# Decoder layer in fp32 on one core: both attentions and the first experts issued in an order written call by call, with the last softmax weighting on POOL

## The reference

```python
x = x + attn(layernorm(x))          # 16 heads of 8, groups of 32 tokens, causal, q and k with rms norm
x = x + xattn(layernorm(x), ctx)    # own layer norm, 16 heads of 64, 64 context rows per batch, w_out, tanh(gate)
x = x + moe(layernorm(x))           # 16 experts of width 128, top 4 of the best 2 of 4 groups, 2 shared experts
# moe: y_e = (silu(x @ gate_e) * (x @ up_e)) @ down_e, weighted by the routing and summed over e
```

## Time and profile before

| | us |
|---|---|
| median of 3 runs | 193.97 (193.88 to 194.04) |
| the profiled execution | 193.8 |
| its span | 192.1 |
| PE busy | 176.5 (92%) |
| DVE busy | 141.4 (74%) |
| POOL busy | 120.1 (63%) |
| ACT busy | 107.6 (56%) |

### The profile page before, as it was taken

How to read it: one execution, slowest core, us unless ns; L and a number is a source line. 1 busy time by engine, 2 the same in 40 slices (tenths; PEclk the granted TensorE clock), 3 DMA queues, 4 the chain that set the end, 5 groups by cost and what they waited for, 6 DMA issues and landing times.

```text
span 192.1 us, 4580 instructions
## 1 busy us (share of the span) xinstructions
PE 176.5 (92%) x1685; PEld 132.8 (69%) x1685; DVE 141.4 (74%) x309; ACT 107.6 (56%) x211; POOL 120.1 (63%) x177
## 2 busy tenths in 40 slices
PE   5899989999799889999987989999999999999992
PEld 5678776667665547677776856666668888888882
DVE  5784485878886896989898869994456776776565
ACT  6458687666774554444585465352346556655550
POOL 4484699855675626665654313017999999998800
PEclk9999999999999999999999999999999999999999
DMA  5986400001113000000000000617993654400003
GB/s 149 306 236 174 123 3 5 2 3 31 31 44 110 3 0 0 0 0 3 2 0 0 3 0 9 249 31 216 367 291 92 212 157 157 137 21 0 0 2 109
DMA packets 17718, 15.75 MB, mean 82 GB/s; under 512 B 2224, under 2 KB 13568, under 8 KB 17568
## 3 DMA queue, kind: packets, MB, share of 16 engines
q1 hardware_dynamic: 16832, 15.13, 25.6%
q10 hardware_dynamic: 864, 0.33, 0.6%
HBM read 14.86 MB, written 0.59 MB: 80 GB/s over the span
## 4 chain that ended last, share of the span: by engine, by line
PE 64%; DVE 13%; ACT 8%; POOL 8%; issue 6%; DVEq 0%; POOLq 0%
PE banks L1488 5%; PE banks L1527 4%; PE banks L1509 4%; PE banks L1514 4%; PE banks L1512 4%; PE banks L1510 4%; PE banks L1513 4%; PE banks L1511 4%; PE banks L1316 3%; POOL kbd L487 3%; PE banks L1531 3%; PE banks L1532 3%; PE banks L1530 3%; DVE sum L1027 3%; DVE mx L1017 2%
## 5 line engine op out<-in xcount | busy, mean ns | idle before, releaser
L770 ACT ACTIVATE s<-banks 128x512 f32<-128x512 f32 x36 | 21.3, 598 | 29.9 <-PE banks L1511 29.6
L495 POOL TENSOR_TENSOR act<-act,vbd 128x512 f32<-128x512 f32 x14 | 22.2, 1587 | 2.6 <-DMA vbd<-comb_rows 1.4
L646 POOL TENSOR_TENSOR gu_lo<-gu_w,gu_hi 128x256 fp32r<-128x256 f32 x14 | 11.3, 810 | 16.1 <-ACT gu_hi L776 16.1
L487 POOL TENSOR_TENSOR kbd<-kbd,rs 128x1024 f32<-128x1024 f32 x7 | 13.3, 1902 | 12.6 <-DVE rs L1031 12.6
L1151 DVE TENSOR_TENSOR act<-s,banks 128x512 f32<-128x512 f32 x20 | 13.6, 685 | 10.1 <-ACT s L770 7.5
L495 POOL TENSOR_TENSOR qk_fold<-qk_fold,vbd 128x512 f32<-128x512 f32 x12 | 19.1, 1600 | 0.8 <-DVE qk_fold L1151 0.4
L1151 DVE TENSOR_TENSOR qk_fold<-s,banks 128x512 f32<-128x512 f32 x16 | 10.9, 687 | 9.2 <-PE banks L1514 5.8
L1509 PE MATMUL banks<-x3hi,gu_lo 128*128 128x512 f32 x36 | 16.7, 465 | 0.3 <-DVE qk_fold L1151 0.3
L764 ACT COPY p2T<-banks 128x512 f32<-128x512 f32 x16 | 8.6, 588 | 14.3 <-PE banks L1476 14.2
L1488 PE MATMUL banks<-vo_fold,p2T 128*128 128x128 f32 x128 | 16.0, 278 | 0.5 <-ACT p2T L764 0.5
L1488 PEld LDWEIGHTS banks<-vo_fold,p2T 128*128 128x128 f32 x128 | 14.9, 191 | 1.3 <-ACT p2T L764 1.1
(11 more groups left out here) (178 smaller groups left out, 466.3 us busy)
## 6 DMA issues: line engine op xcount, KB each, us to landing
vbd<-comb_rows SPq DMA_DIRECT2D x30, 256.0 KB, 3.7
wkv_sb<-in_L_xattn_w_kv_dram SPq DMA_DIRECT2D x1, 1024.0 KB, 8.2
gu_w<-in_L_ffn_gate_w_dram SPq DMA_DIRECT2D x16, 64.0 KB, 2.7
gu_w<-in_L_ffn_up_w_dram SPq DMA_DIRECT2D x16, 64.0 KB, 3.0
vo_fold<-in_L_ffn_down_w_dram SPq DMA_DIRECT2D x1, 960.0 KB, 5.6
wq_sb<-in_L_xattn_w_q_dram SPq DMA_DIRECT2D x1, 512.0 KB, 5.9
wout_sb<-in_L_xattn_w_out_dram SPq DMA_DIRECT2D x1, 512.0 KB, 6.5
x<-in_x_dram SPq DMA_DIRECT2D x3, 128.0 KB, 3.0
```

What stands on the lines that cost most here:

```text
L487: engine.tensor_tensor(p2[:, t % 4, :, :], p2[:, t % 4, :, :], rs2[:, t % 2, :].unsqueeze(2).to_broadcast([P, H2, CTX]), ALU.mult).then_in ...
L495: engine.tensor_tensor(act_of(k), act_of(k), spread[:, j % SPREAD, :], ALU.mult).then_inc(scale_early if j < RING else scale_s, 1)
L770: sc.activation(sil[:, k % 2, :], bank[2 * (k % 2)], ACT.Silu).then_inc(sil_s, 1)
```

## The change

All loops of calls are unrolled, on every engine, and the calls stand in another order. No instruction is added or removed, but one moves to another engine: `norm_p2(7)` from DVE to POOL. SP's queue keeps its order. The core of the diff (lines with one leading sign are those of the diff; "..." stands where calls are left out):

```diff
@@ gpsimd
             norm_scale_pair(2)
+            norm_scale_pair(3)
             rms(0)
-            norm_scale_pair(3)
+            late_constants()
             rms(1)
             causal_mask()
             rms(2)
+            split_down(0)
             value_ones()
             rms(3)
-            late_constants()
-            for i in range(STEPS):
...
+            split_down(1)
+            split_weights(0, 0, 0)
+            split_down(2)
...
+            norm_p2(pool, 6)
+            norm_scale(2, 5)
+            norm_apply(2, 5)
+            norm_p2(pool, 7)
...
@@ vector
                 dve.reciprocal(rs2[:, t % 2, :], sum2[:, t % 2, :]).then_inc(rs2_s, 1)
-                if t == NT - 1:
-
-                    dve.wait_ge(pn2_s, t)
-                    norm_p2(dve, t)
...
             normalize_k(3)
+            mask1(0)
+            max1_sub(0)
             build_kbd(3)
...
+            mask1(3)
+            max1_sub(3)
+            residual1(1)
+            norm_stats(1, 0)
+            norm_y(2)
...
+            residual1(3)
+            norm_stats(1, 2)
+            norm_stats(1, 3)
+            mask1(6)
+            norm_y(4)
...
+            softmax2_max(4)
+            residual2(2)
+            norm_stats(2, 2)
+            softmax2_sum(4)
...
@@ tensor
+            transpose_p2(2)
+            logits(0)
+            output2(2, 0)
+            transpose_xn3(1)
+            output2(2, 1)
+            transpose_p2(3)
+            scores2(6)
+            output2(3, 0)
...
+            down(1)
+            logits(7)
             gate_up(3)
             gate_up(4)
-            down(1)
             transpose_combine(0)
...
+            down(31)
+            down(32)
+            gate_up(35)
             transpose_sum(0)
-            down_last(NS)
+            down(33)
+            down_last(34)
```

More of the change, by code:

```diff
@@ L859, in _ @@
-            copy_p1T(NT - 1)
-            for u in units_of(NT, 0):
-                copy_fold(u)
-            exp2(0)
[L863 to L877, removed]
+            exp1(0)
@@ L1182, in _ @@
             normalize_k(3)
+            mask1(0)
+            max1_sub(0)
             build_kbd(3)
[L1184 to L1192, removed]
+            mask1(1)
+            max1_sub(1)
+            norm_y(0)
+            mask1(2)
+            residual1(0)
@@ new lines, in _ @@
+            max1_sub(2)
+            norm_y(1)
+            mask1(3)
[3 more added lines that the diff above has]
+            norm_y(2)
+            mask1(4)
+            max1_sub(4)
+            residual1(2)
+            mask1(5)
+            norm_y(3)
+            norm_stats(1, 1)
+            max1_sub(5)
+            residual1(3)
[3 more added lines that the diff above has]
+            norm_y(4)
+            residual1(4)
@@ new lines, in _ @@
+            transpose_y(0)
+            scores1(2)
+            transpose_p1(1)
+            project_out(0)
+            fold(("kv", 5))
+            values1(1)
+            scores1(3)
+            fold(("A", 1))
+            transpose_y(1)
+            transpose_p1(2)
+            fold(("kv", 6))
+            project_out(1)
+            scores1(4)
+            values1(2)
+            fold(("A", 2))
+            transpose_p1(3)
+            transpose_y(2)
+            fold(("kv", 7))
+            project_out(2)
@@ new lines, in _ @@
+            scores1(5)
+            values1(3)
+            fold(("A", 3))
+            transpose_y(3)
+            scores1(6)
+            transpose_p1(4)
+            project_out(3)
+            fold(("VW", 0))
+            values1(4)
+            transpose_p1(5)
+            transpose_y(4)
+            project_out(4)
+            fold(("x2", 0))
+            values1(5)
+            fold(("VW", 1))
+            scores1(7)
+            transpose_y(5)
+            transpose_p1(6)
+            project_out(5)
@@ new lines, in _ @@
+            fold(("x2", 1))
+            fold(("VW", 2))
+            values1(6)
+            scores2(0)
+            transpose_y(6)
+            transpose_p1(7)
+            project_out(6)
+            fold(("x2", 2))
+            fold(("VW", 3))
+            values1(7)
+            scores2(1)
+            transpose_y(7)
+            scores2(2)
+            project_out(7)
+            fold(("rw", 0))
+            scores2(3)
+            fold(("x2", 3))
+            transpose_p2(0)
+            output2(0, 0)
@@ new lines, in _ @@
+            scores2(7)
+            logits(2)
+            output2(4, 0)
+            transpose_xn3(3)
+            output2(4, 1)
+            transpose_p2(5)
+            logits(3)
+            gate_up(0)
+            transpose_xn3(4)
+            output2(5, 0)
+            logits(4)
+            output2(5, 1)
+            gate_up(1)
+            transpose_p2(6)
+            output2(6, 0)
+            transpose_xn3(5)
+            output2(6, 1)
+            logits(5)
+            transpose_p2(7)
```

622 lines of the change are left out of this document (436 added, 186 removed).

## The result

| | before | changed |
|---|---|---|
| median, us | 193.88 (5 runs, 193.75 to 194.04) | 198.67 (5 runs, 197.75 to 199.77) |
| profiled execution, its span | 193.8, 192.1 | 197.75, 196.0 |

The change makes the kernel 2.45% slower: ratio 1.0245, interval 1.0203 to 1.0288. I had forecast 193.3 and a range up to 195.5. The profiled execution is the shortest of the five; the median is 0.9 us above it. The mean granted clock of the five executions, shortest first, is 0.991, 0.991, 0.981, 0.983 and 0.981.

The account below looks back on a forecast made before the run. PE was taken as the bound, fully busy from 128 to 186 us, so reordering could win only earlier or at the end. Terms from +2.2 to -1.85 summed to -0.7: span 191.4, median 193.3, range 191.2 to 195.5.

Parts of the forecast that it names:

- step 1: Start: split_down(0), moved ahead on POOL, waits for the down loads and stalls PE at transpose_k(3); +2.2 us.
- step 7: Routing and experts: late routing multiplies delay gate_up(6) and (7), +0.2 us; from there PE is full either way, 0.
- covered by this stall: Edits ahead of 23.8 us: hidden by the load stall up to 2.7 us either way, so priced at nothing.
- Rival D: PE's stand at 23.8 us makes the granted clock fall to 1.2 GHz: 3 us, time 196.3; chance 0.06.
- Steps 2 to 4: First attention rounds -0.7, fourth round with scores1(6) early -0.65, VW folds +0.6, start of second attention -0.4 us.
- Steps 5 and 6: Second attention reordered to 5.05 us a tile, last weighting moved from DVE to POOL: together -1.85 us.
- Rival A: Second attention: exp2 on ACT starts late, a tile costs 5.2 us or more, stall not won back: 195.2; chance 0.25.
- Rival C: Experts: POOL falls behind by one scale_act, 1.6 us on top of the forecast: 194.9; chance 0.11.

Follow-up runs that it names:

- the first part alone: Kernel before with only the changed order up to project_v(3), split_down(0) left behind rms(3): 192.87 us, ratio 0.9948.
- the split alone: Kernel before with only split_down(0) moved between rms(2) and value_ones on POOL: 196.97 us, ratio 1.0170.
- filled gap: Changed kernel with 14 or 32 identity transposes on PE ahead of transpose_k(3): 197.78 us, ratio 1.0186, and 197.82 us, ratio 1.0183.

## Why the prediction was wrong

Two steps failed: the clock in step 1, which I let stand at 1.00, and "from there PE is full either way" in step 7, which I priced at nothing.

**Step 1, the load.** The mechanism of the stall was right to 0.3 us: I had put rqk(3) at 26.1 and transpose_k(3) at 26.55, and the trace has 25.82 and 26.33. But the offset at kv fold 4 was +3.45 and not +2.2. What I had left out is the clock. The calls from transpose_k(3) to the first A fold took 6.22 us where they take 4.81 at 1.00 (2.08 against 1.13 us for one fold, 1.99 against 1.51 for the projection), so 1.4 us of the +3.45 are the low level, and without them about +2.05 would be left, near my +2.2.

That the other edits ahead of 23.8 us are "covered by this stall" was right for the changed kernel, and it hid the better reading: without the stall they are worth 1.1 us (the first part alone), and they made the PE gap longer, 3.80 us against 2.53 with the split alone, since PE finished its earlier work sooner. In these two traces the clock fell behind the longer gap and not behind the shorter, though by their mean clock it fell somewhere in other executions of the split alone too. What a stall covers still lengthens the idle time in front of it.

**Rival D, the clock**, I gave 0.06, because no row of before showed a fall; but none showed a PE gap of that length either, so the rows spoke neither way. Its size was 1.4 us in this trace and not the 3 that I had put; in the trace with a mean clock of 0.981, which three of the changed kernel's five executions have too (0.981 to 0.983), it was 2.4, near my 3. So the price was fair, the chance was not. The Trainium skill (TensorE: Matmul & The Clock Gate, What's actually happening) has idleness gate the clock down, and the traces agree: 0.50 behind gaps of 3.80 and 2.92 us, 1.00 behind 2.53 in another kernel.

**Steps 2 to 4** together were forecast at -1.15 and gave -0.9, but distributed otherwise. A round took 4.05 us (38.54 to 42.59) where I had said 4.0, and the scores1(6) that I had done ahead of VW 0 brought 0.2 and not 0.65. In return norm_y(4) and the VW copies cost nothing; in this stage the changed kernel gained 0.4.

**Steps 5 and 6** were right. The maxima of tiles 3 to 6 on DVE:

```profile
78.01 1.21 DVE L1194 TENSOR_REDUCE mx<-banks 128x16 f32<-128x1024 f32 x1
...
93.30 1.16 DVE L1194 TENSOR_REDUCE mx<-banks 128x16 f32<-128x1024 f32 x1
```

(93.30 - 78.01) / 3 = 5.10 us a tile, against 5.05 forecast and 5.2 before; -1.65 of the forecast -1.85; the weighting ran on POOL for 1.90 us from 104.42 to 106.32, 1.3 later than forecast since all there was later, and was worth 0.7. Rival A didn't happen.

**Step 7** held up to gate_up(7). **The experts** are where the sum failed most: "from there PE is full either way" was worth 2.7 us in the profiled execution, 3.2 to 3.35 between medians. I had gone through the calls with the durations of the old order, in which rest_act took 0.78 to 0.82 us. Those durations belong to the old interleaving with POOL. The sign was there in the kernel before, in rows that I had not weighed:

```profile
151.52 0.92 DVE L1157 TENSOR_TENSOR act_lo<-act,act_hi 128x512 fp32r<-128x512 f32 x1
151.84 1.76 POOL L495 TENSOR_TENSOR act<-act,vbd 128x512 f32<-128x512 f32 x1
152.92 0.69 DVE L1151 TENSOR_TENSOR qk_fold<-s,banks 128x512 f32<-128x512 f32 x1 [0.48 <-PE banks L1514]
153.53 0.69 DVE L1157 TENSOR_TENSOR act_lo<-act,act_hi 128x512 fp32r<-128x512 f32 x1
153.69 1.68 POOL L495 TENSOR_TENSOR qk_fold<-qk_fold,vbd 128x512 f32<-128x512 f32 x1
```

rest_act takes 0.69 or 0.92 us and the product beside it 1.68 or 1.76, while a product with nothing of DVE's beside it takes 1.28 (133.82 in the changed kernel): where DVE is first, POOL pays 0.4. The multiply (L1151, one of its inputs in a bank of PSUM) takes 0.69 us in either kernel, even beside a product. In the changed kernel a product often starts first, and rest_act pays, up to 1.78 us, which is 1.09 more than alone and less than one product. The Trainium skill (SBUF — State Buffer, SBUF: two separate sides) has a rule for this: GpSimd and a VectorE operation with two inputs from SBUF share a pair of ports, the one that starts first holds it for its whole instruction, and the other waits. The traces agree, down to the multiply that is never stretched. By it and the rows a rival could have been priced: 22 rest_act, each longer by at most one product, 1.28 us. Rival C had the right place and the wrong engine: PE's listed waits there are for DVE, which POOL had slowed.

**The median** was another 0.9 above the profiled execution. The clock accounts for that size: the profiled one has a mean clock of 0.991, the median one 0.981, and between traces with 0.991 and 0.981 the price of the fall grew from 1.4 to 2.4 us (no trace of one of the changed kernel's longer executions exists, so for them this is an estimate). Why the fall lasts longer in some executions is open. The first split started at 21.64 in the changed kernel's trace (197.75 us), at 22.02 and 22.55 in the traces with a filled gap (198.98 and 199.82 us); that the landing of the load makes the spread, directly and through the longer gap, is likely, not shown.

## What to carry to other kernels

A wait that is moved forward in a queue onto a load is priced by the load's landing, and its cost passes to everything queued behind it on three engines; look first at what the queue does next, and keep such a call behind the last item that the critical engine needs. The idle time is not the whole price: behind it the low clock cost 1.4 to 2.4 us more here. When an order is rearranged on an engine that is full only because its helpers just keep up, durations of before need not hold: VectorE operations with two SBUF inputs and GpSimd's stretched each other here, and who pays depends on who starts first, so it should be the engine with slack. And a version of many moves is best cut at points where all queues have done the same calls: here that showed two losses of 5.8 and 3.3 us over a gain of 4.3.

## What the runs showed of the hardware

- DVE's subtraction of 128x512 took 0.69 us alone and up to 1.78 beside POOL's product; the product took 1.28 alone and up to 1.76.
- The granted clock fell to 0.50 behind PE gaps of 2.92 and 3.80 us and stayed at 1.00 behind one of 2.53. The calls that take 4.81 us at 1.00 took 7.20 and 6.22 there.
- The down load of 960 KB took 5.4 to 6.3 us to land in the traces with the same SP queue, and 6.9 when eight smaller loads were issued behind it.
